# A transformer layer with multi-query attention: the end of sequence 0 placed in the first steps of sequence 1, and the third feed-forward weight prepared there too

## The reference

```python
q = (x @ Wq + bq).reshape(B, T, H, HD).transpose(0, 2, 1, 3)    # 16 heads of 32
k = (x @ Wk + bk)[:, None]                                      # one key head, one value head
v = (x @ Wv + bv)[:, None]
q, k = _rotary(q, HD), _rotary(k, HD)
attn = softmax(einsum('bhqd,bhkd->bhqk', q, k) / sqrt(HD))
ctx = einsum('bhqk,bhkd->bhqd', attn, v)
x = layernorm(x + ctx @ Wo + bo)
...
def _quantize(w):
    gamma = jnp.mean(jnp.abs(w))
    return jnp.clip(jnp.round(w / (gamma + EPS)), -1.0, 1.0)
hidden = sigmoid(x @ _quantize(w1).T) * (x @ _quantize(w2).T)   # 1408 wide
x = layernorm(x + hidden @ _quantize(w3).T)
```

## Time and profile before

| | us |
|---|---|
| median of 3 runs | 624.04 |
| lowest, highest | 619.8, 626.7 |
| the profiled execution's own time | 625.79 |
| its span | 624.0 |
| PE, DVE, ACT, POOL busy | 551.5, 469.7, 427.3, 292.4 |
| first score of sequence 0, of sequence 1, of sequence 2 (start) | 31.25, 137.26, 268.79 |

### The profile page before, as it was taken

The page is one execution under the profiler, slowest core; times in us unless marked ns, Lnnn a source line. Parts: engine busy times, 40 slices in busy tenths (PEclk is TensorE's granted clock), DMA queues, the critical chain, the costliest instruction groups (busy, mean ns, idle before and its releaser), DMA issues.

```text
span 624.0 us, 9143 instructions
## 1 busy us (share of the span) xinstructions
PE 551.5 (88%) x2964; PEld 273.0 (44%) x2964; DVE 469.7 (75%) x635; ACT 427.3 (68%) x865; POOL 292.4 (47%) x398
## 2 busy tenths in 40 slices
PE   6768878887988999999889999999699999989994
PEld 2444445523444444444444444454344444444441
DVE  1867876748889987998978988799979898435332
ACT  1688777728688888876788987686888898134310
POOL 1308698887625443777455332877355310211001
PEclk9799888998989999999989999999899999999998
DMA  7490535027899998899989997999898989300001
GB/s 295 132 348 2 164 118 174 1 47 153 151 199 203 186 179 151 152 186 185 223 169 215 164 178 137 169 179 201 160 209 163 183 156 182 75 15 35 0 1 67
DMA packets 217103, 92.12 MB, mean 148 GB/s; under 512 B 204384, under 2 KB 205536, under 8 KB 216544
## 3 DMA queue, kind: packets, MB, share of 16 engines
q1 hardware_dynamic: 209952, 77.61, 59.9%
q0 software_dynamic: 6144, 12.60, 9.5%
q10 hardware_dynamic: 960, 1.33, 0.6%
HBM read 20.20 MB, written 4.19 MB: 39 GB/s over the span
## 4 chain that ended last, share of the span: by engine, by line
PE 63%; DVE 12%; ACT 7%; issue 7%; DMA 6%; SPq 3%; POOL 2%; POOLq 0%; DVEq 0%; ACTq 0%
PE a_ps L1245 12%; PE b_ps L1245 6%; PE a_ps L1176 6%; PE s_ps L1258 5%; PE s_ps L1285 5%; PE c_ps L1337 5%; PE e_ps L1245 5%; DVE p_all L1005 4%; PE b_ps L1258 3%; PE c_ps L1323 3%; DVE sh_sb L998 3%; DMA late<-in_w 2%; PE e_ps L1176 2%; DMA xT_sb<-in_xT 2%; PE b_ps L1230 2%
## 5 line engine op out<-in xcount | busy, mean ns | idle before, releaser
L709 ACT ACTIVATE p_all<-s_ps,sh_sb 128x512 f32<-128x512 f32 x192 | 130.0, 682 | 72.8 <-DVE sh_sb L998 72.4
L998 DVE TENSOR_REDUCE sh_sb<-s_ps 128x2 f32<-128x1024 f32 x96 | 116.9, 1217 | 33.5 <-PE s_ps L1285 33.4
L1005 DVE SCALAR_TENSOR_TENSOR p_all<-p_all 128x1024 f16<-128x1024 f32 x96 | 130.6, 1361 | 2.3 <-ACT p_all L717 2.0
L717 ACT ACTIVATE p_all<-p_all 128x1024 f16<-128x1024 f32 x96 | 101.7, 1059 | 2.0
L1245 PE MATMUL a_ps<-late,q 128*128 128x512 f16 x352 | 84.9, 385 | 3.3 <-DVE late L945 1.7
L1285 PE MATMUL s_ps<-k_st,q_st 128*128 128x512 f32 x192 | 80.2, 500 | 7.2 <-ACT p_all L709 4.0
L417 POOL DMA_DIRECT2D q_st<-hi x96 | 49.3, 516 | 64.1 <-ACT hi L643 38.0
L540 POOL TENSOR_SCALAR rstd<-mv 128x1 f32<-128x1 f32 x32 | 7.5, 235 | 142.3 <-DVE mv L965 142.1
L1176 PE MATMUL a_ps<-xT_sb,wq_sb 128*128 128x512 f32 x104 | 57.4, 687 | 11.2 <-DMA wq_sb<-in_wq 6.1
L417 POOL DMA_DIRECT2D q_st<-lo x96 | 47.2, 497 | 13.6 <-DVE lo L908 13.2
L1245 PEld LDWEIGHTS a_ps<-late,q 128*128 128x128 fp8e4 x352 | 31.9, 99 | 47.2 <-issue 8.9
(11 more groups left out here) (147 smaller groups left out, 994.9 us busy)
## 6 DMA issues: line engine op xcount, KB each, us to landing
q_st<-hi POOLq DMA_DIRECT2D x96, 64.0 KB, 3.0
q_st<-lo POOLq DMA_DIRECT2D x96, 64.0 KB, 3.9
late<-in_w SPq DMA_DIRECT2D x2, 2816.0 KB, 11.7
xT_sb<-in_xT SPq DMA_DIRECT2D x8, 512.0 KB, 5.3
late<-in_x SPq DMA_DIRECT2D x4, 1024.0 KB, 6.7
out<-late SPq DMA_DIRECT2D x12, 256.0 KB, 3.0
late<-in_w SPq DMA_DIRECT2D x2, 1408.0 KB, 7.1
q_st<-hi SPq DMA_DIRECT2D x32, 64.0 KB, 2.0
```

The lines of the kernel that those rows point to most:

```text
L709: act.activation(p_pair[n][:, t % 2, :], pair_banks(h * PAIRS + t // 2)[:, t % 2, :], ACT.Exp, bias=sh_sb[:, 2 * n + t % 2:2 * n + t % 2 + ...
L717: act.activation(p_half[n][:, 0, :], p_pair[n].rearrange("p t k -> p (t k)"), ACT.Copy, scale=P_SCALE).then_inc(p_hi, 1)
L998: dve.tensor_reduce(sh_sb[:, 2 * n:2 * n + 2], pair_banks(h * PAIRS + i), AX.X, ALU.min).then_inc(maxed, 2)
L1005: dve.scalar_tensor_tensor(out=p_half[n][:, 1, :], in0=p_pair[n].rearrange("p t k -> p (t k)"), scalar=P_SCALE, in1=p_half[n][:, 0, :], op ...
```

## The change

Names: b is the sequence of the step loop, k its step, h a head.

- Head loop: the turn after head 15 is gone. q0 of sequence 1 is projected in heads 10 and 11, q1 in heads 14 and 15. The key of sequence 1 is projected after head 10 and folded after head 11, in the bank c_ps (counted in kv_filled and kv_drained) and no longer in e_ps; ScalarE's copies of it stand after heads 10 and 11, VectorE's shuffle after head 13 and its halves after head 15. `pairs` and `halves` of q0 stand after heads 12 and 13.
- Step loop of sequence 1: step 0 starts on the scores; behind them stand the four transpositions of head 15 with three blocks of its context. The fourth block, the sums and the value parts follow the scores of step 1. ScalarE's and VectorE's copies of head 15 stand in step 0, `norm_row` in step 1 and `normalise` in step 2.
- The third weight: its sums in steps 4 to 7, its total after step 8, its threshold in step 9, POOL's rounding in two halves, pieces 0 and 2 before stack 8, pieces 1 and 3 after the rotation of q3. Its load is issued after the last stack of sequence 0 and that of xT(1) before head 12's stack. POOL's bias additions for sequence 0 stand in front of stack 3.

```diff
-FIRST_Q_AT = [3, 7, 15]
-FIRST_Q = [(0, 2), (0, 3), (1, 0)]
-ABS_AT = [0, 0, 1, 1, 2, 3, 4, 5, 9, 9, 10, 10]
-TOTAL_AT = [3, 7, 11]
+FIRST_Q_AT = [3, 7, 11, 15]
+FIRST_Q = [(0, 2), (0, 3), (1, 0), (1, 1)]
+ABS_AT = [0, 0, 1, 1, 2, 3, 4, 5]
+TOTAL_AT = [3, 7]
...
             for h in range(HPG + 1, 3 * HPG):
                 stack(sp, 0, h)
+            load_xT(1)
+            for h in range(3 * HPG, H):
+                stack(sp, 0, h)
             sp.wait_ge(rounded, PIECES)
             sp.dma_start(stage[2], w3).then_inc(w_ffn[2], 16)
-            for h in range(3 * HPG, H):
-                stack(sp, 0, h)
-            load_xT(1)
...
                 inverse_std(b - 1, 0, 3)
+                if b == 1:
+                    pool.wait_ge(thr_step, 2 * 3)
+                    round_weight(2, 0, 0)
+                    round_weight(2, 2, 1)
                 stack(pool, b, 8)
                 stack(pool, b, 9)
                 cosines(b, "q3")
+                if b == 1:
+                    round_weight(2, 1, 2)
+                    round_weight(2, 3, 3)
...
@@ ScalarE, step loop
+                    if (b, k) == (1, 0):
+                        move(H - 1, 0)
                     exps(b, h, 2 * i)
+                    if (b, k) == (1, 0):
+                        move(H - 1, 2)
                     exps(b, h, 2 * i + 1)
...
-                    if k == 2 and b > 1:
+                    if k == (2 if b > 1 else 1):
                         norm_row(b - 1, HG - 1)
+                    if b == 1 and k in (4, 5, 6, 7):
+                        abs_sum(2 * SUMS + (4, 5, 6, 7).index(k))
...
@@ VectorE, head loop and step loop
+                    if h == 13:
+                        pairs(1, "k")
+                    if h == 15:
+                        halves(1, "k")
...
+                    if (b, k) == (1, 0):
+                        move(H - 1, 1)
+                        reciprocals(0, HG - 1)
+                        move(H - 1, 3)
+                    if (b, k) == (1, 2):
+                        normalise(0, HG - 1)
...
@@ TensorE
+            def next_key_parts():
+                pe.wait_ge(ctx_done, 2)
+                for half in range(2):
+                    pe.wait_ge(xT_in[half], 2 * 16)
+                parts(c_ps, wk_sb, kv_filled)
+
+            def next_keys():
+                pe.wait_ge(kv_drained, 4)
+                pe.matmul(c_ps[:, :], eye4_sb, th[:, :], start=True, stop=True).then_inc(kv_filled, 1)
+
+            def last_of_first():
+                turn(H - 1, 0)
+                turn(H - 1, 1)
+                first_context(HG - 1, [0])
+                turn(H - 1, 2)
+                first_context(HG - 1, [1])
+                turn(H - 1, 3)
+                first_context(HG - 1, [2])
...
                     score(b, *divmod(k, PAIRS))
+                    if (b, k) == (1, 0):
+                        last_of_first()
+                    if (b, k) == (1, 1):
+                        pe.wait_ge(pt_dve, 2 * H)
+                        first_context(HG - 1, [3])
+                        turn_sums(0, HG - 1)
+                        value_parts(1)
                     for name, s in beside(b, k):
                         use(name, s)
+                    if b == 1 and k == 8:
+                        total(2)
```

More of the change, by code:

```diff
@@ L122, in beside @@
     return [(use, b + of) for use, of in uses if not (use[:2] == "dn" and b + of < 0)
-            and not (b == 1 and (use, of) in (("sums3", -1), ("ctx3", -1)))]
+            and not (b == 1 and (use, of) in (("sums3", -1), ("ctx3", -1), ("vp", 0)))]
 def up_at(b, k):
@@ L524, in cosines, with round_weight @@
                     pool.tensor_tensor(rot[:, 1, :], rot[:, 0, :], rot[:, 1, :], ALU.add).then_inc(rotated, 1)
[L526 removed]
+            def round_weight(n, c, place=None):
                 w, q = piece(stage[n], c, PIECES), piece((q1, q2, q3)[n], c, PIECES)
[L529 removed]
+                steps = 2 * (n * PIECES + (c if place is None else place))
                 pool.tensor_scalar(w, w, thr[:, n, 0:1], ROUND, ALU.mult, ALU.add).then_inc(pool_step, 1)
@@ L566, in _ @@
                 round_weight(1, c)
-            pool.wait_ge(thr_step, 2 * 3)
-            for c in range(PIECES):
-                round_weight(2, c)
-            for t in range(TT):
-                add_bias(0, t)
             cosines(1, "q0")
@@ L576, in _ @@
                 stack(pool, 1, h)
+            for t in range(TT):
+                add_bias(0, t)
             for b in range(1, B):
@@ L748, in first_heads @@
             def first_heads():
-                for h in range(H + 1):
-                    if h < H:
-                        first_exps(h, 0)
+                for h in range(H):
+                    first_exps(h, 0)
                     if h >= 1:
                         move(h - 1, 0)
-                    if h < H:
-                        first_exps(h, 1)
-                        first_exps(h, 2)
+                    first_exps(h, 1)
+                    first_exps(h, 2)
                     if h % HPG == 1 and h > HPG:
@@ L766, in first_heads @@
                         unit(s, f"q{g}")
+                    if h == 11:
+                        unit(1, "k")
                     if h in ABS_AT:
@@ L839, in _ @@
             first_heads()
-            key_copy(1)
-            norm_row(0, HG - 1)
-            unit(1, "k")
             for b in range(1, B):
@@ L1030, in first_heads @@
             def first_heads():
-                for h in range(H + 1):
-                    if h < H:
-                        first_max(h, 0)
-                        first_max(h, 1)
+                for h in range(H):
+                    first_max(h, 0)
+                    first_max(h, 1)
                     if h >= 1:
@@ L1094, in heads @@
                         value_halves(b)
+                    if b == 1 and k == 9:
+                        thresholds(2)
                     if k == 9:
@@ L1357, in first_heads @@
             def first_heads():
-                for h in range(H + 1):
+                for h in range(H):
                     full, after = h % HPG == 0 and h > 0, h % HPG == 1 and h > HPG
-                    if h < H:
-                        first_score(h, 0)
-                        first_score(h, 1)
-                        first_score(h, 2)
-                        first_score(h, 3)
+                    first_score(h, 0)
+                    first_score(h, 1)
+                    first_score(h, 2)
+                    first_score(h, 3)
                     if after:
```

78 lines of the change are left out of this document (41 added, 37 removed).

## The result

| kernel | median of the runs | ratio to before, 95% interval |
|---|---|---|
| before | 622.93 us (20 runs beside the change) | 1 |
| changed | 620.17 us (20 runs) | 0.9955 [0.9936, 0.9975] |

The change wins 2.8 us, 0.45%. The prediction said 7.7. The time of 620 is inside the range of 610.5 to 621.5. The change stays within 1%, to which 26% had been given; most of the chance had gone to more. What happened stands nearest to the first rival, contention that takes most of the gain, but most of it was lost in another place than that rival had it.

A forecast was written before the change was run, and what follows sets the result against it. TensorE was taken to bound the step loop; before it every engine waits for another in turn. The terms summed to 11.0 - 0.3 - 3.0 = 7.7 us won, so a median of 616 us, range 610.5 to 621.5.

The forecast's parts named there:

- the first rival: Steps 9 to 17: low halves meeting a POOL pass wait most of 1.4 us; 3.2 us won, 620.8; chance 22%.
- Terms 1 to 3: Heads 9 to 15: 1.5 us won, then 1.5 and 1.0 lost; sequence 0 ends at 123.2 instead of 122.2.
- Term 4: Seam to step 4's exponentials: scores of step 0 at about 123.8, exponentials at 141.9 against 152.90; 11.0 us won.
- term 3: Head 13: VectorE's hi, lo and shuffle cost 1.0 us; key's halves, at most 1.4 us, fall beside the last exponentials.
- Term 6: Weight and x loads, threshold: no cost; late x would hold up bias additions, stack 3 and the q1 rotation.
- One of the prediction's own signs of being wrong: Steps 0 to 2 of sequence 1: the prediction is wrong if VectorE and not TensorE sets them.
- The low clock: Steps 0 to 4 of sequence 1: no stretch at a lower granted clock; 1.6 us of it taken off step 3 to 4.
- Term 5: Steps 4 to 7: the third weight's sums on ScalarE, 5.5 us, mostly covered by idle time; 0.3 us lost, bounds 0 and 2.8.
- Term 7: Steps 9 to 15: POOL's moved rounding of the third weight delays VectorE; 3.0 us lost, bounds 0 and 8.
- The sign given for it: Low halves of steps 9 to 15 at up to 2.6 us, mean over all 96 up by about 0.1 us.
- The third rival: Stacks 8 to 11 behind the rounding: POOL's queue becomes the bound, step 18 waits 9 us, 632 us; chance 6%.

The follow-up runs named there:

- e1: Changed kernel with POOL's four bias additions of sequence 0 moved from in front of stack 3 to behind it; ratio to before 0.9877.
- e8: Changed kernel with five matmuls nobody reads issued on TensorE in its wait ahead of step 0's scores of sequence 1; ratio to before 0.9907.
- e2: Changed kernel without the third weight's rounding (its twelve POOL passes work on one column only); ratio to before 0.9890.
- e4: Kernel before with only the third weight's load, sums, total, threshold and rounding placed as in the change; ratio to before 1.0064.
- e12: e5 with the four bias additions of sequence 0 behind stack 4 instead of stack 3; ratio to before 0.9961.
- e13: Changed kernel with sequence 0's four bias additions one each behind stacks 1, 2, 3 and the rotation of q1; ratio to before 0.9821.
- e5: e1 with the third weight's sums behind heads 9, 9, 10, 10 and its first rounding half ahead of stack (1, 0); ratio to before 0.9940.
- e9: e1 with two of POOL's bias additions of sequence 1, ahead of stacks 10 and 11, moved behind stack 11; ratio to before 0.9865.
- e10: Changed kernel with two of POOL's bias additions of sequence 1, ahead of stacks 10 and 11, moved behind stack 11; ratio to before 0.9983.

## Why the prediction was wrong

1. **Terms 1 to 3, up to the last exponential: the sum right, in part by luck.** Head 9 to the last exponential was to become 1.0 us longer; it went from 40.25 us to 41.33 (121.56 - 81.31; 120.92 - 79.59). One by one, heads 9 and 10 won 1.1 us (1.5 forecast), head 11 lost 1.0 (1.5), head 13 lost 1.9 (1.0), and heads 14 and 15, put at nothing, won 0.7.
2. **Term 4, the seam, is the step that failed**, at its first line, "Scores of step 0 at about 123.8". They came at 126.25, though head 9 had begun 1.7 us earlier than before. The line takes over a price from term 3: the key's halves as "two operations like lo, at most 1.4 us", from a row with POOL quiet. They took 5.2 (0.88 and 4.34), beside four additions of POOL in a row. Term 6 had these additions at exactly this place and asked only whether their input would be late, not what they would do to the VectorE operation beside them. 11.0 us was priced, 4.8 won. e1, without that collision, won 10.6, so the rest of the term's working holds. Of the 5.8 between, 4.1 are the longer wait (5.25 against 1.13) and 2.25 the clock (e8), less about 0.5 by which steps 1 to 4 are shorter in the changed kernel than in e1. One of the prediction's own signs of being wrong was that VectorE and not TensorE sets steps 0 to 2; for step 0 it came true.
3. **The low clock** was said to be gone from steps 0 to 4. It came back, for TensorE was idle 5.25 us ahead of the block.
4. **Term 5, the sums: right as far as seen.** Step 4 to 8 takes 17.85 us, before 18.73, so no loss shows. Term 6, loads and threshold: POOL's additions waited for no load, and nothing is seen of the threshold.
5. **Term 7, the rounding: right in kind, too small.** 3.0 priced with bounds 0 and 8; 4.0 by e2, and by e4 4.0 for the weight's whole move. The profiled pair lost only 2.8 between steps 4 and 20 because without rounding the changed kernel needs 68.5 us there (e2) and the one before 69.25, a gain of 0.8 that the sum did not count. The sign given for it, a mean of all 96 low halves up by about 0.1 us, did not come: it went from 1.36 to 1.35, for the kernel before had slow ones too (2.86 at 152.78, 2.12 at 201.16).
6. **The rivals.** Contention did take most of it, as the first rival said, but at the key, where the rival did not look. Its low halves of steps 9 to 17 are the smaller part. The third rival's wait did not happen in the changed kernel (hi of q3 at 213.18 waited for nothing) and did in e1 and e8.
7. **The rule of the skill.** The Trainium skill, "SBUF — State Buffer", section "SBUF: two separate sides", would let an operation wait for the rest of one GpSimd operation that began first, here at most 1.27 us. The rows agree for the rounding passes (1.84 for 0.69, 2.19 for 1.22) and not for four additions in a row: 4.34, 5.55, 6.24, 4.01 and 3.41 us. Nor had the additions begun first: by the profile's start times the subtraction was 0.08 us ahead (121.76 and 121.84), the low half in e12 0.23. Over the 16 traces 21 operations with two SBUF inputs began ahead of the GpSimd arithmetic that then went first, all during a DMA issue. The measurement decides.

## What to carry to other kernels

When a change puts a VectorE operation from SBUF to SBUF onto the path, look at what stands in GpSimd's queue at the same microsecond, and price all of GpSimd's arithmetic that follows there without a wait or other work in between, not one instruction. Move the row away from that operation, or split it: the same four additions made this kernel 0.8% faster behind stack 3 (e1) and 1.3% faster one by one (e13), and the two can't be told apart. Then look at what the row meets in its new place (e12). Add the clock to a wait of TensorE of some 5 us, and ask which queue binds next once the steps come earlier.

## What the runs showed of the hardware

- A VectorE operation with two SBUF inputs that met four GpSimd additions of 1.27 us in a row was let in late, and not at the first gap. The 0.69 us subtraction ended at 126.10, behind three of them: these end at about 125.5, and the fourth took 1.73. In e5 it was let in behind four, where the rotation's multiplication took 1.73, and in e12 the 1.22 us low half behind four. The low halves of e9 and e10 (3.41 and 3.42 us) began in the second of four and went in ahead of the last.
- Where only two GpSimd operations followed each other, a held operation went in behind the first, in all 62 cases (2.72 us for 1.22 in e1).
- A VectorE copy with one SBUF input and SBUF output was held too (4.01 us in e1; 1.66 in e13, beside one addition of 1.29), while the copy out of PSUM just ahead of it, with an addition beside it, kept its 0.68 us.
- A VectorE operation with two SBUF inputs that began during a GpSimd DMA issue was held only where arithmetic followed the issues at once: 53 of 202 such, none of the other 304.
- The hold goes both ways: GpSimd's second pass took 2.20 us beside a low half, 1.36 elsewhere.
- TensorE idle for 5.25 us came back at a granted clock of 0.65 for 8.4 us, and after a wait of 3.93 us the clock was 0.50 from 186.04 to 189.70; idle for 1.13 us (e1), or busy in the wait (e8), it was at 1.00.
